# Passing half of the batch from one attention to the next early: the stages between two attentions of a fused transformer kernel

## The reference

```python
x = L0_attn_x
x = _layernorm(x + _L0_attn_ref(x, Wq, Wk, Wv, Wo))       # 16 heads of 8, 4 k/v groups, ALiBi
x = _layernorm(x + _L0_ffn_ref(x, w_freq_real, w_freq_imag, bias))   # ifft(fft(x) @ w) + bias
x = _layernorm(x + _L1_attn_ref(x, W_qkv, W_out))         # segments of 128, every 2nd key
x = _layernorm(x + _L1_ffn_ref(x, sim, gates, p_q, p_k, p_v, p_o))   # 16 experts, full attention

# in _L1_attn_ref, with scale = 8 ** -0.5:
qs = q.reshape(B, H, nseg, seg, Dh)
ks = k.reshape(B, H, nseg, seg, Dh)[:, :, :, ::dil]
scores = einsum('bhnqd,bhnkd->bhnqk', qs, ks) * scale
out = einsum('bhnqk,bhnkd->bhnqd', softmax(scores), vs)
return inverse_permutation(out) @ W_out
```

## Time and profile before

| | |
|---|---|
| runs, us | 799.52, 801.78, 807.97; median 801.78 |
| profiled execution | 806.35 us, span of the core 804.5 us |
| busy, share of the span | PE 689.3 us (86%), DVE 636.0 (79%), ACT 445.1 (55%), POOL 155.7 (19%) |
| mean granted clock of TensorE | 0.915 of full |
| last `outputs0` of the first attention ends | 371.45 us |
| last product between the attentions ends | 412.83 us |
| first `seg_max` of the second attention | 422.42 us |
| second attention's last output copied | 481.62 us |

### The profile page before, as it was taken

One profiled execution on the slowest core, in us unless ns is written; L12 is line 12 of the kernel. 1 busy time (PEld: TensorE's weight loads), 2 busy tenths in 40 slices (PEclk: granted clock), 3 DMA queues, 4 the chain that ended last, 5 costly groups with the idle time before them and its releaser, 6 DMA issues.

```text
span 804.5 us, 16665 instructions
## 1 busy us (share of the span) xinstructions
PE 689.3 (86%) x5878; PEld 441.6 (55%) x5878; DVE 636.0 (79%) x1149; ACT 445.1 (55%) x974; POOL 155.7 (19%) x287
## 2 busy tenths in 40 slices
PE   7499888888888888899955988499999998998883
PEld 5233333333333333335533766499999997996652
DVE  2688999999999999942574647889999994554996
ACT  3058999999999999984641436202111114454442
POOL 6400000000000000003331007601111122123563
PEclk9558999999999999999985669589999998999998
DMA  7711111111111110002556500000000000000000
GB/s 197 222 22 32 32 32 31 32 32 31 33 31 32 32 31 3 2 3 68 142 140 172 156 16 1 0 1 0 2 0 0 0 0 1 0 0 1 15 13 26
DMA packets 19401, 31.87 MB, mean 40 GB/s; under 512 B 4952, under 2 KB 12504, under 8 KB 18040
## 3 DMA queue, kind: packets, MB, share of 16 engines
q1 hardware_dynamic: 17992, 29.42, 13.9%
q0 software_dynamic: 1344, 1.58, 0.7%
HBM read 23.25 MB, written 7.34 MB: 38 GB/s over the span
## 4 chain that ended last, share of the span: by engine, by line
PE 52%; ACT 18%; issue 10%; DVE 10%; DMA 5%; SPq 2%; POOL 2%; DVEq 0%; POOLq 0%; ACTq 0%
ACT probs L1166 16%; PE ps_hi L749 13%; PE ps_lo L998 7%; PE ps_lo L1000 6%; PE ps_lo L999 6%; PE ps_hi L763 4%; PE ps_hi L1058 3%; DMA q_rep<-mrow 2%; DVE probs L1747 2%; DVE mx L1465 2%; PE ps_hi L1049 1%; SPq L385 1%; ACT mrow L1121 1%; PE ps_hi L810 1%; PE ps_hi L930 1%
## 5 line engine op out<-in xcount | busy, mean ns | idle before, releaser
L1465 DVE TENSOR_REDUCE mx<-ps_lo 128x2 f32<-128x1024 f32 x256 | 306.2, 1224 | 12.2 <-PE ps_lo L726 9.0
L1166 ACT ACTIVATE probs<-ps_hi 128x512 f32<-128x512 f32 x512 | 278.0, 596 | 38.4 <-PE ps_hi L749 25.8
L763 PE MATMUL ps_hi<-probs,v_blk 128*32 128x256 f32 x2048 | 168.2, 401 | 5.6 <-ACT mrow L1121 5.5
L749 PE MATMUL ps_hi<-q,k 28*128 28x512 f32 x512 | 132.0, 509 | 26.9 <-ACT probs L1166 13.0
L726 PE MATMUL ps_lo<-k,q 26*128 26x512 f32 x512 | 135.7, 526 | 7.0 <-DVE mx L1465 4.2
L1681 DVE SCALAR_TENSOR_TENSOR tok_cur<-ps_lo,w_cur,tok_cur 128x384 f32<-128x384 f32 x240 | 127.6, 608 | 6.3 <-PE ps_lo L1000 4.7
L749 PEld LDWEIGHTS ps_hi<-q,k 28*128 28x128 f32 x512 | 49.5, 187 | 139.5 <-ACT probs L1166 117.7
L998 PE MATMUL ps_lo<-w_hi,op_hi 128*128 128x384 f32 (+1 forms) x304 | 108.1, 356 | 19.8 <-DVEq L1642 10.1
L999 PE MATMUL ps_lo<-w_lo,op_hi 128*128 128x384 f32 (+1 forms) x304 | 105.4, 347 | 0.0
L1000 PE MATMUL ps_lo<-w_hi,op_lo 128*128 128x384 f32 (+1 forms) x304 | 105.4, 347 | 0.0
L763 PEld LDWEIGHTS ps_hi<-probs,v_blk 128*32 128x32 f32 x2048 | 42.3, 109 | 72.5 <-ACT probs L1166 58.5
(11 more groups left out here) (225 smaller groups left out, 842.8 us busy)
## 6 DMA issues: line engine op xcount, KB each, us to landing
q<-q_parts SPq DMA_DIRECT2D x30, 192.0 KB
q_rep<-q_parts SPq DMA_DIRECT2D x8, 576.0 KB
k<-k_parts SPq DMA_DIRECT2D x32, 96.0 KB
k_rep<-k_parts SPq DMA_DIRECT2D x24, 96.0 KB
q_parts<-qk_hi SPq DMA_DIRECT2D x8, 256.0 KB, 4.9
q_parts<-qk_p SPq DMA_DIRECT2D x12, 128.0 KB, 3.1
xa<-in_L_attn_x SPq DMA_DIRECT2D x4, 256.0 KB, 3.9
q_parts<-qk_lo SPq DMA_DIRECT2D x4, 256.0 KB, 6.3
```

Source lines behind the costliest of these rows:

```text
L749: mm = pe.matmul(bank(4 + (2 * n + a) % 3), k0[rows, k_at:k_at + P], q0[rows, h * QN:(h + 1) * QN], start=True, stop=True)
L763: mm = pe.matmul(o_bank()[32 * r:32 * r + 32, 0:OW], v_all[:, at:at + 32], probs0[:, n % P_RING, r * OW:(r + 1) * OW], start=(kb == 0), st ...
L1166: act.activation(probs0[:, n % P_RING, a * QN:(a + 1) * QN], bank(4 + (2 * n + a) % 3), ACT.Exp).then_inc(s0_free, 1)
L1465: dve.reduce_max(mx2[:, j % 2, :, i, kh], bank(2 * (m % 2), 2).rearrange("p (a n) -> p a n", a=2), AX_X).then_inc(max0_done, 1)
```

## The change

- In the last 14 steps of the first attention TensorE also carries quad 0 through `att_T`, `wo_products`, `ffn_T`, `ffn_products` and `x2_T`, and quad 1 up to `wo_products`. In these steps VectorE does what ScalarE did between (ScalarE is at the exps): copies, and the normalisation of quad 0.
- A quad is no longer four neighbouring tiles but every second tile of its batch (`tile(q, t)`), so that half of the heads' transposed columns are enough for it; `heads_T` and `heads0` work in halves of 8 heads and two PSUM banks. Each quad keeps two banks: `flip_bank(q)` for what is transposed, `res_bank(n, q)` for sums.
- The residual of the Fourier layer is put into `m_sb` (plus the identity); the bias is one product in the single-pass type (`share`, `bias_r`). The scale of q is put into the weights by GpSimd. k and v are computed from the kept positions alone (`xs`), so `select` goes, and k's product has 256 columns instead of 512.
- ScalarE writes the first bf16 part straight from PSUM, and `split` on VectorE has three operations instead of four.
- SP loads `load_rep(0)` to `load_rep(3)` before batch 1's stores. The expert weights come as 16 pieces of 256 KB: four after `load_mrow(1)`, three after each `load_mrow(s + 2)` of the loop.

```diff
+WE, PIECES = 4, 16
@@ banks
+        def half_banks(b, f, part):
+            return bank(4 * b + (2 if f or part else 0), 2)
+        def flip_bank(q):
+            return bank(2 * q)
         def res_bank(n, q):
-            return bank(q if n == 1 else 4 + q)
+            return bank(2 * q + 1 if n < 2 else 4 + q)
+        def tile(q, t):
+            return q // 2 * KB + q % 2 + 2 * t
@@ SP
-            sp.wait_ge(ot0_ps, 2 * NB)
-            for n, p in enumerate((p_q, p_k, p_v)):
-                sp.dma_start(big[:, 0:E * W3].rearrange(...)[:, :, n * D:(n + 1) * D], ...).then_inc(ld_we, 16)
-            sp.dma_start(big[:, E * W3:].rearrange(...), ...).then_inc(ld_we, 16)
             for q in range(2):
                 store_q1(q)
+            sp.wait_ge(const_set, 9)
+            sp.wait_ge(s0_ps, NU)
             stored1(0)
-            sp.wait_ge(const_set, 12)
-            sp.wait_ge(s0_ps, NU)
             for s in range(2):
                 load_rep(s)
+            for s in range(2, RING):
+                load_rep(s)
             for q in range(2, NQ):
                 store_q1(q)
             load_mrow(0)
-            for s in range(2, RING):
-                load_rep(s)
             load_mrow(1)
+            sp.wait_ge(ot0_ps, 2 * NQ)
+            for i in range(RING):
+                load_piece(i)
             stored1(1)
             for s in range(NS - RING):
                 sp.wait_ge(seg_s_ps, 2 * (s + 1))
                 load_rep(s + RING)
                 load_mrow(s + 2)
+                for i in range(3):
+                    load_piece(RING + 3 * s + i)
@@ TensorE, new helpers
+            def att_T(q):
+                pe.wait_ge(ot0_read, 2 * q + 2)
+                for t in range(QUAD):
+                    mm = pe.transpose(flip_bank(q)[:, t * P:(t + 1) * P], xT[...], ident_sb[:])
+                mm.then_inc(at_ps[0], 1)
+                add_rows(res_bank(0, q), xa[:, tiles(q), :])
+            def ffn_T(q):
+                pe.wait_ge(ln_out[0], q + 1)
+                tiles_T(xb, q, flip_bank(q)).then_inc(ft_ps, 1)
+                pe.matmul(res_bank(1, q), share[:], bias_r[:].unsqueeze(1).broadcast_to([P, QUAD, D]),
+                          start=True, stop=False)
+            def qkv_products(q):
+                pe.wait_ge(xT_sb[1], q + 1)
+                pe.matmul(flip_bank(q), w_qkv1[:, 0:D], xq, start=True, stop=True)
+                pe.matmul(res_bank(1, q)[:, 0:QN // 2], w_qkv1[:, D:2 * D], xs[:, q % 2, :], start=True, stop=True)
+                for t in range(QUAD):
+                    for odd in range(2):
+                        mm = pe.matmul(values[KSEG * odd:KSEG * (odd + 1), t * KSEG:(t + 1) * KSEG],
+                                       xs[:, q % 2, t * KSEG:(t + 1) * KSEG], w_v[:, :, odd, :],
+                                       start=True, stop=True, tile_position=(0, KSEG * odd))
@@ TensorE, after the steps of the first attention
+            qkv_products(0)
+            ffn_T(1)
+            heads_T(1, 0, 0, 8)
+            ffn_products(1)
+            heads_T(1, 0, 8, 16)
+            att_T(2)
+            wo_products(2)
+            heads_T(1, 1, 0, 8)
+            x2_T(1)
+            heads_T(1, 1, 8, 16)
+            qkv_products(1)
+            att_T(3)
+            ffn_T(2)
+            wo_products(3)
+            ffn_products(2)
+            ffn_T(3)
+            x2_T(2)
+            ffn_products(3)
+            qkv_products(2)
+            x2_T(3)
+            qkv_products(3)
@@ ScalarE
+            normalise(0, 1, xb)
+            qkv1(0)
+            ft_copy(1)
+            at_copy(2)
+            normalise(1, 1, xa)
+            x2_copy(1)
+            qkv1(1)
+            normalise(0, 2, xb)
...
@@ VectorE
-            norm(0, wo_ps[0])
-            norm(1, fm_ps)
...
+            heads0(2, 0)
+            stats(1, 1, fm_ps)
+            heads0(2, 1)
+            shift(1, 1)
+            split(0)
+            stats(0, 2, wo_ps[0])
+            heads0(3, 0)
+            shift(0, 2)
+            heads0(3, 1)
+            split(1)
+            stats(0, 3, wo_ps[0])
...
```

More of the change, by code:

```diff
@@ L519, in _, with layer1_constants, second_parts @@
             blocks(NS * KB, NT * 8)
+            def layer1_constants():
+                pool.wait_ge(ld_w1, 5 * 16)
+                pool.tensor_scalar(w_qkv1[:, 0:D], w_qkv1[:, 0:D], scale, None, ALU.mult).then_inc(w1_scaled, 1)
+                pool.wait_ge(ld_bias, 32)
+                pool.tensor_scalar(share[:], ones[:], 1.0 / 64, None, ALU.mult).then_inc(bias_set, 1)
+                pool.tensor_copy(bias_r[:], bias_sb[:]).then_inc(bias_step, 1)
+                pool.wait_ge(bias_step, 1)
+                pool.tensor_tensor(bias_r[64:P, :], bias_sb[64:P, :], bias_r[64:P, :].bitcast(F32),
+                                   ALU.subtract).then_inc(bias_set, 1)
+                pool.wait_ge(bias_set, 2)
+            def second_parts(first, last):
+                for n in range(first, last):
+                    at = slice(n * WC, (n + 1) * WC)
+                    pool.wait_ge(w_hi_set, n + 1)
+                    pool.tensor_tensor(w_lo[:, at], big[:, at], w_hi[:, at].bitcast(F32), ALU.subtract).then_inc(
+                        w_lo_set, 1)
             for j in range(NH):
@@ L768, in heads_T @@
             def heads_T(b, f, first, last):
-                if first == 0:
-                    if b or f:
-                        pe.wait_ge(ot0_read, (0, 1, 2, 2)[2 * b + f])
-                    if not b and not f:
+                part = first // 8
+                if first % 8 == 0:
+                    if f:
+                        pe.wait_ge(ot0_read, 4 * b + 2 + part)
+                    elif b:
+                        pe.wait_ge(s0_free, 2 * NU)
+                    else:
                         pe.wait_ge(max0_done, NU)
+                    if b and part:
+                        pe.wait_ge(o0_free, NH)
@@ L792, in _ @@
                     max_T((n + 5) // KB)
-                at = n - (NU - AHEAD + 1)
-                if 0 <= at < 12 and at % 6 < 4:
-                    heads_T(0, at // 6, 4 * (at % 6), 4 * (at % 6) + 4)
+                k = n - (NU - AHEAD)
+                if 1 <= k <= 4:
+                    heads_T(0, 0, 4 * (k - 1), 4 * k)
+                elif k == 5:
+                    att_T(0)
+                elif k == 6:
+                    heads_T(0, 1, 0, 4)
+                    wo_products(0)
+                elif 7 <= k <= 9:
+                    heads_T(0, 1, 4 * (k - 6), 4 * (k - 5))
+                elif k == 10:
+                    ffn_T(0)
+                elif k == 11:
+                    att_T(1)
+                    ffn_products(0)
+                elif k == 12:
+                    wo_products(1)
+                elif k == 15:
+                    x2_T(0)
+            qkv_products(0)
[19 more added lines that the diff above has]
+            qkv_products(3)
             def heads_tile(t, source):
@@ L888, in seg_max @@
+                    pe.wait_ge(at_sb[1], q + 1)
+                    quad_products(bank(4 + q), attT[:, q % 2, :], w).then_inc(wo_ps[1], 1)
             def seg_max(s, h):
@@ L1207, in qkv1 @@
-                vb = v_blk[:].rearrange("p (g r c) -> p g r c", g=NT, r=8)[:, q * QUAD:(q + 1) * QUAD]
-                vp = bank(6 + q % 2).rearrange("p (g r two d) -> p g r two d", g=QUAD, r=8, two=2)
-                copy(vb[0:KSEG, :, :, 0:DH], vp[0:KSEG, :, :, 0, :])
-                copy(vb[KSEG:P, :, :, 16:16 + DH], vp[KSEG:P, :, :, 1, :]).then_inc(v_sb[1], 1)
-            for q in range(NQ):
-                attT_copy(q, bank(q), at_ps[0], at_sb[0], wo_ps[0])
-            normalise(0, 0, xb)
@@ L1528, in _ @@
-            select(0)
-            select(1)
-            for q in range(NQ):
-                split(q, QN + QN // 2)
-                if q + 2 < NQ:
-                    select(q + 2)
+            heads0(0, 0)
+            heads0(0, 1)
+            at_copy(0)
+            stats(0, 0, wo_ps[0])
+            heads0(1, 0)
+            shift(0, 0)
+            normalise(0, 0, xb)
+            heads0(1, 1)
+            ft_copy(0)
+            at_copy(1)
+            stats(1, 0, fm_ps)
+            stats(0, 1, wo_ps[0])
@@ new lines, in _ @@
+            shift(1, 0)
+            normalise(1, 0, xa)
+            shift(0, 1)
+            x2_copy(0)
+            heads0(2, 0)
[9 more added lines that the diff above has]
+            stats(0, 3, wo_ps[0])
+            shift(0, 3)
+            stats(1, 2, fm_ps)
+            shift(1, 2)
+            stats(1, 3, fm_ps)
@@ L1536, in seg_max @@
+            shift(1, 3)
+            split(2)
+            split(3)
             def seg_max(s):
```

315 lines of the change are left out of this document (152 added, 163 removed).

## The result

The kernel after the change is **slower**: 815.18 us (median of 4, 811.99 to 819.02) against 801.47 for the kernel before beside it, a ratio of 1.0162 with a 95% interval of 1.01 to 1.0224, or 13 us. The profiled execution has a span of 813.5 us (before: 804.5).

A forecast was written before the change was run, and what follows sets the result against it. Bounds taken: the compute chain between the attentions, then the second attention's DMA queues. Segment 5 at 445.5 + 3 x 7.7 = 468.6 against 465.75, +2.9 us, took the median from 801.78 to 804.8 us; range 795 to 813.

The forecast's parts named there:

- the rounds with pieces: Second attention, segments 2 to 5: three weight pieces lengthen each round from 5.7 to 7.7 us, three rounds +6.0.
- The tail: Last steps of the first attention: the work moved in makes it end 5.6 us later, at 377.0.
- The chain: Between the attentions: the reordered compute brings seg_max(0) to 422.0 against 422.42, a gain of 0.4 us.
- The 64 x 64 products: Eight products in qkv_products, between the attentions: taken as 1.0 us, bounds 0.5 and 1.8.
- Rival 2: Between the attentions: TensorE's clock falls after 3.6 us idle, seg_max(0) at 426, result 809; chance 0.26.
- Before the rounds: Start of the second attention: scores of segment 2 at 444.5 to 446.5 against 448.6, 3 us earlier.
- Rival 1: Second attention: pieces fill idle DMA engines, rounds stay 5.7 us, segment 5 4 us earlier, 796 to 798; chance 0.18.
- Without the weights, segment 5 would stand 5 us earlier: Second attention: the weights, free of charge before, take back a gain of 5 us at segment 5.
- The rest unchanged: Second attention after segment 5: nothing changes, two pairs of maxima, 15.9 us to the end.

The follow-up runs named there:

- e4: Kernel after plus products nobody reads in TensorE's idle stretches between the attentions, to hold its clock; ratio 1.0112.
- e7: Kernel after with the weights issued early and quads 0 and 1 moved back out of the first attention's last steps; ratio 1.0087.
- e1: Kernel after with the expert weights never loaded; 800.1 us, ratio 0.997.
- e5: Kernel after with the sixteen weight pieces issued early and filling products between the attentions; ratio 0.9942.
- e9: Kernel after with filling products, six pieces issued early, four ahead of quad 1's stores, six behind the last maxima; ratio 0.9933.
- e8: Kernel before with only the sixteen weight pieces, issued where the kernel after issues them, in place of its whole loads; ratio 1.0163.
- e2: Kernel after with the same sixteen pieces issued earlier on the same queue, before the second attention; 801.51 us, ratio 0.9966.
- e13: Kernel after with the same sixteen pieces in the same rounds, issued from ScalarE's queue instead of SP's; ratio 1.0134.

## Why the prediction was wrong

The step that failed is the term for the rounds with pieces: 7.7 us each, at most 8.5, where 9.2 was measured. The direction was among its rivals, and the forecast missed the time by 10 us. By its steps:

- **The tail, +5.6**: measured 5.7. **The chain, -0.4**: right at full clock; with the clock held (e4) `seg_max(0)` stands at +69.33, -0.5 against before. It was right on the way too: on the old execution's clock e4's `ffn_T(3)` starts at 405.7, and I had 406.1. (The old chain is 51.0 us long, 371.45 to 422.42, not the 50.5 that I wrote; the 0.4 stands.) The 64 x 64 products took 0.69 of the 1.0 that I took. The tail pays for itself (e7).
- **Rival 2** happened as it was described, idle time of 3.57 us (I had 3.6) behind `ffn_products(2)` and a granted 0.50 from there. Priced 4 us, measured 3.2 by e4. It should have been in the forecast: with 3.6 us of idle time there, and a fall in the trace of before in a like stretch, 0.26 was too low a chance.
- **Before the rounds**: on the old execution's clock the scores of segment 2 came at 449.8 (446.42 + 3.38); I had 445.5. Of these 4.3 us the held clock of e4 takes off 2.6 (+94.61 against +97.22); 1.7 stay, in the stretch where the first four pieces run.
- **The rounds with pieces**, taken 7.7, upper bound 8.5, measured 9.2: three rounds added 4.5 us more than I had given them. Two things were mis-sized. The piece was priced at the 290 GB/s of a load that ran alone, 2.7 us a round; the difference between the rounds with and without pieces is 3.6 (e1), 218 GB/s. And the round without pieces, which 7.7 implies to be 5.0, was 5.6 (e1). The upper bound used the same 2.7 us, so it could not hold the time.
- **Rival 1**, that the pieces fill idle DMA engines: wrong. The share of 0.53 at 137 GB/s was not room for another 0.79 MB a round; the mix took up to 1.01 at 213 GB/s.
- **Without the weights, segment 5 would stand 5 us earlier**: in e1 it stood 0.6 earlier than before (+112.57 against +113.17), with the clock held in e5 2.0, and in e9, where also fewer pieces stand ahead of the replicated loads, 4.2. So the gain was there, but the clock and the queues ahead of segment 0 each had a part of it.
- **The rest unchanged, 15.9**: 16.4.

On the old execution's clock the forecast puts the end of the span at 807.4 (804.5 + 2.9), and it came at 816.9 (813.5 + 3.38). The 9.5 us between are 4.3 before segment 2, 4.5 in the rounds and 0.8 behind them. Of the two parts of the change, the weights' new place explains the loss by itself (e8: 1.0163; e2, without it: 0.9966). Had the prediction compared it with the old place, 15 us of transfers under stages without any, it could have said so: it did name this cost, and gave it 2.0 us a round (7.7 against 5.7) where 3.5 were measured.

Open stays why loads and pieces together take more of the DMA engines than apart. By the earlier trace rows loads alone have a full share at some 260 GB/s (137 at 0.53) and the old weights at some 275 (290 at 1.05); over the three rounds full share means some 220 (183 at 0.83). Open too is why the engines' mean share stays at 0.83 while TensorE waits for a transfer in every round. The rule that the prediction quoted from the Trainium skill ("DMA: Bandwidth & Descriptors", "Why a DMA increments its semaphore by 16 and not by 1") would make it an uneven spread over single engines; no row here shows single engines.

## What to carry to other kernels

A transfer that nobody waits for is free only where nobody waits for another one. Put it where the DMA row of the profile's page is at 0, and look first at who waits for the transfers behind it. Price it in a mixed stage by the GB/s of a mixed stage, not of a load that runs alone. And when a wait for a single buffer shows up behind a late transfer, ask whether the buffer makes the transfer late or the transfer the buffer: two halves moved the wait (18.1 us) and not the end.

## What the hardware showed that I had not expected

- 256 KB pieces in packets of 512 bytes (8448 packets for 4.2 MB in e13) moved at 290 GB/s when they ran alone (398 to 404 us of e2), as fast as the whole loads of before in packets of 2 KB (290).
- TensorE at half clock can be busy for the whole of a stretch and still be granted 0.50, in the stretches of e2:

```profile
442.00:448.00 6.00, 6.00 (x97) 4.80 (x97) 3.13 (x6) 2.05 (x2) 0.00 (x0) 0.50 0.61 160
```

- Filling products kept the clock at 1.00 through waits of 3.6 us at no cost to the chain: 7 of 256 columns, 3.19 us.
